# A constant 128x512 matmul in front of each score unit of the third layer

## The reference

```python
q_rope = _apply_rope(q, sin, cos); k_rope = _apply_rope(k, sin, cos)
att_num = jnp.exp(jnp.einsum('bhqd,bhkd->bhqk', q_rope, k_rope) * scale)
att_den = jnp.sum(jnp.exp(jnp.einsum('bhqd,bhkd->bhqk', q, k) * scale), axis=-1, keepdims=True)
y = jnp.einsum('bhqk,bhkd->bhqd', att_num / att_den, v)
h = y @ w_out.T + x                                        # then a layer norm
...
h = jax.nn.gelu(jnp.einsum('nd,edh->enh', xt, w1) + b1[:, None, :], approximate=False)
y = jnp.einsum('enh,ehd->end', h, w2) + b2[:, None, :]      # 8 experts of 64, top 2
```

## Time and profile before

| | |
|---|---|
| median of three runs | 2250.33 us (2248.04 to 2252.85) |
| the profiled execution, time | 2246.13 us |
| its span, first to last instruction | 2244.3 us |
| PE busy, share of the span | 1596.0 us (71%) |
| PE's weight loads | 792.8 us (35%) |
| DVE busy | 1235.2 us (55%) |
| ACT busy | 1039.4 us (46%) |
| POOL busy | 222.2 us (10%) |
| mean granted TensorE clock | 0.782 |
| third layer | from 1173.7 us to about 1690 us of the span |

### The profile page before, as it was taken

How to read it: one execution, slowest core, us unless ns; L and a number is a source line. 1 busy time by engine, 2 the same in 40 slices (tenths; PEclk the granted TensorE clock), 3 DMA queues, 4 the chain that set the end, 5 groups by cost and what they waited for, 6 DMA issues and landing times.

```text
span 2244.3 us, 24308 instructions
## 1 busy us (share of the span) xinstructions
PE 1596.0 (71%) x8520; PEld 792.8 (35%) x8520; DVE 1235.2 (55%) x2493; ACT 1039.4 (46%) x1569; POOL 222.2 (10%) x208
## 2 busy tenths in 40 slices
PE   5667657767698788788886767677674456877777
PEld 2444434434454444444442322222223042222222
DVE  4977959859774654745553324232215727355371
ACT  3856938748413123131247666576660031523415
POOL 0431413404200000000000000000000211000000
PEclk8887978879799999898996657576666575868768
DMA  5000000000111002010043203021001041211100
GB/s 219 1 1 0 0 0 0 0 0 0 43 47 51 8 2 57 1 51 8 2 114 111 71 14 99 14 68 46 1 1 42 31 114 41 61 40 37 54 23 6
DMA packets 73990, 83.09 MB, mean 37 GB/s; under 512 B 8764, under 2 KB 70716, under 8 KB 73276
## 3 DMA queue, kind: packets, MB, share of 16 engines
q1 hardware_dynamic: 72856, 79.60, 11.7%
q0 software_dynamic: 1024, 2.10, 0.3%
HBM read 50.47 MB, written 31.20 MB: 36 GB/s over the span
## 4 chain that ended last, share of the span: by engine, by line
PE 42%; DVE 29%; ACT 12%; issue 12%; DMA 2%; POOL 1%; SPq 1%; DVEq 0%; ACTq 0%; POOLq 0%
PE ps L975 9%; DVE neg_max L1637 6%; PE ps L699 6%; PE ps L687 5%; PE ps L686 4%; ACT scratch L1230 4%; DVE mixture_sum L1382 3%; ACT ps L1213 2%; PE ps L845 2%; DVE gated L1356 2%; DVE scratch L1485 2%; DVE hidden L1360 2%; PE ps L984 1%; ACT tanh L1089 1%; DVE scratch L1474 1%
## 5 line engine op out<-in xcount | busy, mean ns | idle before, releaser
L1230 ACT ACTIVATE scratch<-ps 128x1024 f32<-128x1024 f32 x336 | 333.9, 1020 | 283.3 <-PE ps L945 142.7
L975 PE MATMUL ps<-scratch,values 128*32 128x512 f32 (+3 forms) x1536 | 224.7, 673 | 18.4 <-ACT scratch L1230 10.1
L1637 DVE TENSOR_REDUCE neg_max<-ps 128x2 f32<-128x1024 f32 (+2 forms) x224 | 224.9, 1064 | 16.9 <-PE ps L890 16.7
L1650 DVE COPY head_out<-ps 128x512 f32<-128x512 f32 x48 | 33.2, 691 | 338.0 <-PE ps L975 337.8
L1810 POOL TENSOR_TENSOR scratch<-scratch 128x512 f32<-128x512 f32 x128 | 160.2, 1273 | 361.2 <-DVE scratch L1485 361.2
L1089 ACT ACTIVATE tanh<-ps 128x512 f32<-128x512 f32 x88 | 52.5, 597 | 302.9 <-PE ps L687 302.9
L699 PEld LDWEIGHTS ps<-weights_even,hidden 128*128 128x128 f32 (+1 forms) x960 | 149.1, 228 | 96.0 <-issue 53.8
L699 PE MATMUL ps<-weights_even,hidden 128*128 128x128 f32 (+1 forms) x960 | 157.2, 316 | 33.3 <-DVE mixture_sum L1382 33.3
L1213 ACT ACTIVATE ps<-ps 128x512 f32<-128x512 f32 x256 | 150.7, 589 | 63.3 <-PE ps L934 63.2
L1480 DVE TENSOR_TENSOR_SCAN scratch<-scratch 128x512 f32<-128x512 f32 x128 | 175.6, 1410 | 1.4 <-ACT scratch L1149 1.4
L687 PE MATMUL ps<-xnt_sequence,weights_even 128*128 128x512 f32 x256 | 151.4, 682 | 0.0
(11 more groups left out here) (268 smaller groups left out, 2555.6 us busy)
## 6 DMA issues: line engine op xcount, KB each, us to landing
scratch<-parts_scratch SPq DMA_DIRECT2D x288, 96.0 KB, 2.3
parts_scratch<-weights_even SPq DMA_DIRECT2D x192, 128.0 KB, 2.4
weights_odd<-in_l SPq DMA_DIRECT2D x1, 4224.0 KB, 28.2
weights_even<-in_l SPq DMA_DIRECT2D x1, 4096.0 KB, 17.2
weights_odd<-in_l SPq DMA_DIRECT2D x1, 4096.0 KB, 12.6
slots_scratch<-weights_even SPq DMA_DIRECT2D x2, 1280.0 KB, 6.3
scratch<-in_sel SPq DMA_DIRECT2D x1, 1024.0 KB, 6.3
slots_scratch<-xn SPq DMA_DIRECT2D x1, 1024.0 KB, 9.5
```

The costliest lines, as they stand in the source:

```text
L975: mm = pe.matmul(ps[32 * i:32 * i + 32, PV, q0:q0 + n], lhs, buf[:, slot, col:col + n], start=first_, stop=True, skip_group_check=True)
L1230: act.activation(dst, src, ACT.Exp).then_inc(q[l, "exp_done"], 1)
L1637: ins = dve.tensor_reduce(dst, ps[:, base:base + 2, col:col + n], AX.X, ALU.max, negate=True)
```

## The change

In the third layer, ahead of each score unit, PE waits until ACT has read bank `UP` for the latest expert step (`up_read`, kept when the step is issued), then issues one matmul of `eyeb` with the first 512 columns of `c16` into that bank. Nothing reads the result. Then the score unit follows with its waits as before. There are 64 such units in a turn, 256 in all.

```diff
                         if l == 1:
                             pe.wait_ge(*mi_read)
                         up(l, b, n)
+                        up_read = (q[l, "hidden_ready"], start[l, "hidden_ready"] + b * NF[l] + n + 2)
                         if l == 1:
                             mi_read = (q[l, "hidden_ready"], start[l, "hidden_ready"] + b * NF[l] + n + 2)
...
                     elif what == "b":
+                        if l == 2:
+                            pe.wait_ge(*up_read)
+                            pe.matmul(ps[:, UP, :], eyeb, c16[:, 0:T], start=True, stop=True)
                         scores_b(l, b, n)
```

## The result

The changed kernel takes 2236.57 us in the median of four runs (2234.21 to 2240.67) beside 2251.59 us for the kernel before on the same chip. The ratio is 0.9934, with a 95% interval of 0.991 to 0.9959: 15 us faster, where I had forecast 10 us slower. That lies inside my range of 2232 to 2280, but on the other side of no change, and within a microsecond of the time that rival B gave (2236). The match with B's figure is partly luck: B asked for a turn clock above 0.85, and the profile has 0.77 to 0.80.

A forecast was written before the change was run, and what follows sets the result against it. It took PE and ACT to alternate as bound, neither full. Fillers 8.4 minus clock return 5.4 made 3.0 us a turn, over 3.5 turns 10 us slower: 2256 profiled, 2260 us median, range 2232 to 2280.

The forecast's parts named there:

- rival B: Third layer: the clock's return outweighs the fillers, half the slow pieces turning fast; 2236 us, chance 0.26.
- The bound, and where the filler stands: Third layer: PE and ACT alternate, no engine full; fillers are covered where PE waits for ACT, added where PE comes late.
- The price of one: Each filler on the path ahead of a score unit costs 0.33 us at the fast clock, 0.54 at the slow.
- The new wait: Wait for ACT's read of bank UP, biting at most 16 times behind `f` steps; taken as 0, bounds 0 to 3 us.
- How many lie on the path: 19 of a turn's 64 score units have no ACT wait right before them; their fillers cost 8.4 us a turn.
- rival D: Third layer's clock doesn't move, as constant products or too few filled gaps may not count; 2282 us, chance 0.06.
- My sign for a count that is too high: In the profile after, ACT's idle time falling would mean fewer fillers on the path than the 19 a turn counted.
- What the clock may give back: Third layer: some slow stretches, not most, turn fast, returning 5.4 us a turn; turn clock 0.72 to 0.78.
- B's break-even: Third layer: the clock's return outweighs the fillers from 8.4 / 22.5, some 37% of the slow pieces turning fast.
- The page's rule: Keep TensorE busy without gaps; by it alone fillers would hold the fast level through nearly the whole turn, 2193 us.
- the far end of B: Score stretches never fall back and all slow pieces turn fast, 57 us over the layer; 2193 us, chance 0.04.

The follow-up runs named there:

- e_late_rows32: Kernel before plus a 32-row filler only ahead of the 167 score units not behind two other units; ratio 1.0300 to the kernel before.
- e_wait_only: Changed kernel with the filler matmul left out and the new wait kept; 2251.12 us beside 2250.96 for the kernel before, ratio 1.0000.
- e_rows32: Changed kernel with the filler on 32 rows instead of 128, at all 256 places; ratio 1.0284 to the kernel before, 63 us slower.
- e_free_tail: Kernel before plus full fillers at the 89 units behind two units and eight in each turn's tail; 2215.08 us, ratio 0.9856.

## Why the prediction was wrong

- **The bound, and where the filler stands**: right. PE's waits for ACT before units shrank by more than half (80 to 35 us), the filler is nearly covered behind two units (0.05 us each) and often on the path elsewhere (in `e_late_rows32` a filler has 0.32 us of the chain on average).
- **The price of one**: right, 0.32 and 0.54 us against 0.33 and 0.54.
- **The new wait**: right in its effect. PE's weight loader does wait for the Gelu in the first `f` step of each turn, four times in all, but the array reaches the unit with the `values` part before it just done, and ACT is loading its table meanwhile; `e_wait_only` gives 1.0000.
- **How many lie on the path**: too few. 19 a turn make some 66, and the chain of the changed kernel goes through 89. By 19 a turn and no return (rival D) it would have been 32 us; the 32-row fillers measured 63. I kept the chain of the kernel before and counted on it, though each filler that makes PE later moves the chain from ACT to PE and uncovers the next: ACT fell from 101 to 49 us of the chain in `e_rows32`. Part of the 63 is clock that the narrow filler itself cost. With the return there, the same shift was mild: 53 us came onto the chain and 28 us of ACT left it, 25 net beside my 8.4 x 3.5 = 29. So this term hardly moved the sum. My sign for a count that is too high, ACT's idle time falling, did appear (118.7 to 112.2 us of waits for scores) and misled: it can't tell a lower cost from a higher return.
- **What the clock may give back**: this is the step that failed and turned the sign. I listed 5.4 us a turn, 19 over the layer, on the ground that a filler only displaces other work where PE is full, and expected "not most" of the slow stretches to turn. The clock rose to 0.77 to 0.80, at or just above the upper end of the 0.72 to 0.78 that I named, and on the chain of the changed kernel PE's own work outside scores and fillers fell by 31 us: `values` by 13, `down` by 8, `up` and the projections by 6, the rest by 4. That is 12 us more than my list. With 4 us less of net cost it makes 16 of the 16.5 us between the forecast (10 us slower) and the profiled stretch (6.5 faster). The list priced single pieces of one turn's chain; slow `values` parts and `down`s between them weren't on it. Narrow against full filler at the same places differ by more, some 77 us (1.0284 against 0.9934 to 0.9939), but there the clocks are 0.61 and 0.79, so the narrow one's own loss is in that figure. B's break-even was 37% of the slow pieces and some 38% of the slow time turned fast. So B had the direction and the mechanism; its size, 14 us from half of the slow pieces, was reached by the medians and not by the profiled stretch.
- **The page's rule**: the far end of B, by the Trainium skill ("TensorE: Matmul & The Clock Gate", "Why this matters for your kernels": keep TensorE busy, avoid idle gaps), did not come. `e_rows32` fills the same places and has 0.61 at 87% busy, and 0.50 over 26 us without a gap; here the measurement decides against gaps alone as the ground.
- **D**, that products of constants might not count, fell: zeros and constants raised the clock.

What stays open: the profiled executions show 6.5 to 7.6 us of the gain in the stretch, the unprofiled medians 14 to 15 us in all. The profiled execution of the kernel before was 4.2 us under the median of its first runs, that of the changed kernel 4.1 above its own, which accounts for 8 us of difference in what was sampled. Outside the stretch every profiled execution here took 1737 to 1743 us, so no variant moved the rest of the program by more than that spread; where the unprofiled runs differ I can't see.

## What to carry to other kernels

Where TensorE runs at its slow level though it is busy, look at how many rows of the array its matmuls use: here a filler that reads nothing late and works on 128 rows bought back part of the fast level for the work around it. Put it only where the queue is going to wait anyway, here behind two score units, and dose it there: 89 places with two fillers each gave more than twice the gain of 256 places with one. To forecast it, price the kernel at both levels whole rather than adding up pieces of the old chain, and expect the chain to move: a filler on it is free as far as it takes the place of another engine's work.

## What the runs showed of the hardware that I had not expected

- A matmul with one column of weights raised the granted clock as far as one with 128 (0.77 against 0.79), one with 32 rows instead of 128 lowered it (0.61 against 0.66 without any).
- Narrow work in the gaps did harm beyond its time: with 32-row fillers the `up` matmuls averaged 1042 ns instead of 861, because more of them ran at the slow level.
- Fillers right behind each other are cheaper than one among score units: the eight in the tails of `e_free_tail` start 0.43 us apart at the slow and 0.22 at the fast clock, each with its own weight load, where a single one takes 0.54 and 0.32.
- The runs of the kernel before are spread from 2240.9 to 2253.3 us within one series, and the executions with the higher mean clock are the short ones (0.786 at 2240.92, 0.778 at 2252.74).
